# Two fp32 one-hots instead of one bf16 one-hot in the edge loop of the third graph layer

## The reference

```
z = h @ W_func.T
e = leaky_relu(concat(z[edge_src], z[edge_dst], w) @ W_att.T, 0.01)
m = segment_max(e, edge_dst)
alpha = exp(e - m[edge_dst]);  alpha /= segment_sum(alpha, edge_dst)
agg = segment_sum(alpha[:, None] * z[edge_src], edge_dst)
h_new = relu(h @ W_self.T + agg)          # h itself for nodes without an edge
x = x + h + h_new
```

## Time and profile before

| what | value |
|---|---|
| median of 3 runs | 8807.85 us (8803.87 to 8810.25) |
| profiled execution, its own time | 8805.21 us |
| its span | 8803.1 us |
| mean granted TensorE clock | 0.83 |
| DVE busy over the span | 5511.9 us (63%) |
| POOL busy over the span | 5197.2 us (59%) |
| PE busy over the span | 5993.1 us (68%) |
| ACT busy over the span | 3064.8 us (35%) |

### The profile page before, as it was taken

The page is one execution under the profiler, slowest core; times in us unless marked ns, Lnnn a source line. Parts: engine busy times, 40 slices in busy tenths (PEclk is TensorE's granted clock), DMA queues, the critical chain, the costliest instruction groups (busy, mean ns, idle before and its releaser), DMA issues. The chain is left out here.

```text
span 8803.1 us, 115446 instructions
## 1 busy us (share of the span) xinstructions
PE 5993.1 (68%) x29150; PEld 4494.9 (51%) x29150; DVE 5511.9 (63%) x14431; ACT 3064.8 (35%) x8921; POOL 5197.2 (59%) x5085
## 2 busy tenths in 40 slices
PE   0266787775259766656598999974477775574499
PEld 0133555553248534444477777763355553453487
DVE  8787888887656566665544434346577777435444
ACT  0111888886422210000233333321244444313322
POOL 0274666665567667777577777742677771433422
PEclk9687999998579987777699989877689886786699
DMA  9412655665147533333111111116433344463364
GB/s 303 152 52 80 172 172 170 175 174 150 37 152 213 163 99 101 101 102 102 35 28 30 26 29 31 26 27 200 115 103 104 104 102 116 155 214 91 115 199 163
DMA packets 655611, 1031.12 MB, mean 117 GB/s; under 512 B 134978, under 2 KB 462066, under 8 KB 654780
## 3 DMA queue, kind: packets, MB, share of 16 engines
q0 software_dynamic: 238656, 527.35, 22.3%
q1 hardware_dynamic: 390636, 444.00, 16.0%
q10 hardware_dynamic: 25744, 53.10, 2.0%
HBM read 806.11 MB, written 225.75 MB: 117 GB/s over the span
## 5 line engine op out<-in xcount | busy, mean ns | idle before, releaser
L4092 POOL DMA_INDIRECT gat_edges_rows<-gat_table,gat_room x1080 | 1171.4, 1085 | 366.4 <-issue 327.9
L2570 POOL DMA_INDIRECT l_edges_ring<-pairs,first_room x832 | 841.8, 1012 | 525.6 <-issue 243.1
L2132 POOL DMA_INDIRECT l_sum_rows<-l_feats,back_room x832 | 826.7, 994 | 279.8 <-issue 241.9
L2152 PE MATMUL l_sum_o<-l_sum_rows,l_sum_s 128*128 128x256 f32 x1664 | 616.2, 532 | 442.3 <-DVE l_sum_s L2163 206.2
L2621 ACT ACTIVATE l_edges_ring<-l_edges_ring,l_edges_weight 128x64 f32<-128x64 f32 x3328 | 816.5, 336 | 0.0
L2152 PEld LDWEIGHTS l_sum_o<-l_sum_rows,l_sum_s 128*128 128x128 f32 x1664 | 416.3, 264 | 635.8 <-DVE l_sum_s L2163 306.6
L2693 PE MATMUL l_edges_o<-l_edges_ring,l_edges_sf 128*128 128x260 f32 x1664 | 534.5, 427 | 148.8 <-DVE l_acc L2826 140.9
L3723 ACT ACTIVATE m_ffn_ht<-m_ffn_hp,m_ffn_b1t 128x256 f32<-128x256 f32 x592 | 280.7, 475 | 868.4 <-PE m_ffn_hp L3691 868.1
L2174 DVE TENSOR_TENSOR l_acc<-l_acc,l_sum_o 128x256 f32 x832 | 350.0, 421 | 346.6 <-PE l_sum_o L2152 256.6
L3701 PE MATMUL m_ffn_yp<-m_ffn_w2b,m_ffn_ht 128*128 128x256 f32 x2368 | 546.6, 384 | 29.2 <-ACT m_ffn_ht L3723 28.5
L3691 PE MATMUL m_ffn_hp<-m_ffn_xt,m_ffn_w1b 128*128 128x256 f32 x2368 | 548.7, 385 | 5.8 <-DVE m_ffn_xt L3738 3.0
(11 more groups left out here) (868 smaller groups left out, 14612.4 us busy)
## 6 DMA issues: line engine op xcount, KB each, us to landing
sorted_rows<-count_main_zero ACTq DMA_DIRECT2D x1, 51858.0 KB, 237.8
l_proj_taken<-m_by_node SPq DMA_DIRECT2D x56, 768.0 KB, 7.4
m_ffn_xs<-sorted_rows SPq DMA_DIRECT2D x144, 258.0 KB, 3.5
m_ffn_w1b<-in_L_ffn_w SPq DMA_DIRECT2D x32, 1024.0 KB, 6.2
m_ffn_w2b<-in_L_ffn_w SPq DMA_DIRECT2D x32, 1024.0 KB, 5.1
m_ffn_w1b<-in_L_ffn_W SPq DMA_DIRECT2D x56, 512.0 KB, 4.5
m_ffn_w2b<-in_L_ffn_W SPq DMA_DIRECT2D x56, 512.0 KB
m_by_node<-gat_edges_ys SPq DMA_DIRECT2D x96, 256.0 KB
```

Of the source, the lines that this page charges most:

```text
L2132: pool.indirect_dma_start(rows[:, slot, j, :], None, table, bass.IndirectOffsetOnAxis(ap=L.src[:, t:t + 1], axis=0)).then_inc(got[slot], 16)
L2152: pe.matmul(o[:, j, 0:D], s4[:, q % S4, j, :], rows[:, slot, j, :], start=True, stop=True).then_inc(out_done, 1)
L2570: pool.indirect_dma_start(rows(q, 0, 2 * D)[:, j, :], None, table, bass.IndirectOffsetOnAxis(ap=L.src[:, t:t + 1], axis=0)).then_inc(got[q ...
L4092: pool.indirect_dma_start(rows[:, slot, j, :], None, table, bass.IndirectOffsetOnAxis(ap=L.src[:, q * B + j:q * B + j + 1], axis=0)).then_ ...
```

## The change

The ring `s8` goes. In its place stand `early`, two slots in fp32, and `late`, four slots in fp32. Together they take as many bytes as `s8` did (12 slots of 2 bytes an element against 6 of 4 bytes). VectorE now makes each quad's one-hot twice: `first_onehot`, lag 2, into `early`, for `exclude`; and `second_onehot`, lag 7, into `late`, for `turn_s` and `weigh_s`. `turn_s` reads the upper halves of the fp32 words as bf16 (1.0 and 0.0 lie there whole), which is every other 2-byte element. `first_onehot` waits for the mask of two quads before, `second_onehot` for the weighing of four quads before. A semaphore `late_ready` is added.

In VectorE's step s the order of the plain functions is now: `second_onehot(s-7)`, `first_onehot(s-2)`, `score(s-2)`. Before it was: `score(s-2)`, `onehot(s)`. The generators follow in both.

```diff
-        s8 = ph.sb("s8", [P, U, B, P], BF16)
+        SA, SB = 2, 4
+        early = ph.sb("early", [P, SA, B, P])
+        late = ph.sb("late", [P, SB, B, P])
+        late_high = late[:].rearrange("p s b k -> p (s b k)").bitcast(BF16).rearrange(
+            "p (s b k half) -> p s b k half", s=SB, b=B, k=P, half=2)[:, :, :, :, 1]
...
+        late_ready = ph.sem("late_ready")
...
-                    act.activation(far[:, q % 2], s8[:, slot], ACT.Identity, bias=minus_far[:],
+                    act.activation(far[:, q % 2], early[:, q % SA], ACT.Identity, bias=minus_far[:],
                                    scale=FAR).then_inc(far_ready, 1)
...
                     act.wait_ge(ex_ready, q + 1)
+                    act.wait_ge(late_ready, q + 1)
...
-                        act.activation(ws[:, q % 2, j, :], s8[:, slot, j, :], ACT.Identity,
+                        act.activation(ws[:, q % 2, j, :], late[:, q % SB, j, :], ACT.Identity,
                                        scale=ex[:, q % 2, j, :]).then_inc(ws_ready, 1)
...
-                    pe.wait_ge(s_ready, q + 1)
+                    pe.wait_ge(late_ready, q + 1)
...
-                        ins = pe.transpose(stp[:, j, :], s8[:, slot, j, :], core.ident_b[:])
+                        ins = pe.transpose(stp[:, j, :], late_high[:, q % SB, j, :], core.ident_b[:])
...
-                def onehot(q, slot):
-                    if q >= U:
-                        dve.wait_ge(ws_ready, (q - U + 1) * B)
-                    dve.tensor_tensor(s8[:, slot], bc(core.row[:], 1, [P, B, P]),
-                                      bc(L.dst[:, q * B:(q + 1) * B], 2, [P, B, P]), ALU.is_equal).then_inc(s_ready, 1)
+                def onehot(out, q):
+                    return dve.tensor_tensor(out, bc(core.row[:], 1, [P, B, P]),
+                                             bc(L.dst[:, q * B:(q + 1) * B], 2, [P, B, P]), ALU.is_equal)
+
+                def first_onehot(q, slot):
+                    if q >= SA:
+                        dve.wait_ge(far_ready, q - SA + 1)
+                    onehot(early[:, q % SA], q).then_inc(s_ready, 1)
+
+                def second_onehot(q, slot):
+                    if q >= SB:
+                        dve.wait_ge(ws_ready, (q - SB + 1) * B)
+                    onehot(late[:, q % SB], q).then_inc(late_ready, 1)
...
-                steps(dve, n, [(0, onehot), (2, score), (2, split), (4, update), (5, refresh), (9, exponent),
+                steps(dve, n, [(2, first_onehot), (7, second_onehot), (2, score), (2, split), (4, update), (5, refresh), (9, exponent),
                                (10, add)], **whole)
```

## The result

The changed kernel takes 8821.08 us (median of 20 runs, 8805.09 to 8829.89), the kernel before 8803.28 us (20 runs, 8792.74 to 8814.38). The ratio is 1.0017, with a 95% interval of 1.001 to 1.0023: slower by 0.17%, or 17.8 us between the medians; the interval is 9 to 20 us. The forecast was 8831 us, +26 us, in a range of 8806 to 8872.

The account below looks back on a forecast made before the run. The prediction took POOL's back-to-back gathers as the bound. Gather delays of +23 us and a tail of +3 us, +26 us on the profiled execution's 8805.21 us, gave 8831 us, range 8806 to 8872 (own range 8818 to 8850).

Parts of the forecast that it names:

- The bound: In the loop, POOL issues gathers back to back, DVE follows the landed rows and the other engines follow DVE.
- A second comparison is free on DVE: The added one-hot's 1.13 us a step lies under DVE's 2.0 us wait for rows before `score`.
- The fp32 output, ScalarE's fp32 reads and the strided loads at nothing: fp32 one-hots on DVE, `exclude` and `weigh_s` on ACT, `turn_s` weight loads on PE: each taken as 0 us.
- One gather's wait per pair, to the end of the first one-hot: A gather starting inside the first one-hot ends 0.82 us behind that one-hot's end; one delay per pair.
- 0.55 us a step for even phases: Mean gather delay from a pair in the loop, against 0.31 before; over 97 steps +23 us.
- The part for gathers held through a pair: Within the delay per pair: 2 in 82 gathers held 1.3 us longer, adding 0.03 us.
- the second rival: Port held through the whole pair in one of four kinds of step: +46 us on top, 8877 us; chance 0.14.
- The tail: Behind the last gather, five more steps make a `second_onehot`: +3 us, between 0 and 5.7.
- DVE's wait for rows, 1.2 us a step: DVE's wait before `score` in the loop was to fall from 2.0 to about 1.2 us a step.
- without the one-hot inside (1.13): Removing the one-hot behind `score` shortens that part of DVE's step by 1.13 us; two in front add 2.26.
- The fourth rival: DVE becomes the bound if its steps grow by more than 1.3 us; 8900 us with 2 us more; chance 0.03.
- rival 1: Pairs meet gathers at kind phases, delay 0.25 to 0.45 us a step; 8802 to 8822 us, say 8812; chance 0.26.

Follow-up runs that it names:

- pair_behind: Changed kernel with both fp32 one-hots issued directly behind `score` instead of in front; 8822.92 against 8821.96 us for the kernel before, ratio 1.0003.
- one_ahead: Kernel before with its single bf16 one-hot moved to lag 2, in front of `score`; 8827.69 against 8821.96 us, ratio 1.0000.
- bf16_pair: Changed kernel with both one-hots in bf16, so `turn_s` loads contiguous weights; 8833.73 against 8821.96 us for the kernel before, ratio 1.0013.
- by_tile: Kernel before with its single 1024-element comparison made as eight short `tensor_scalar` comparisons of 128 elements; 8794.36 against 8821.96 us, ratio 0.9969.
- three_in_front_3: Changed kernel with `first_onehot` computed twice in a row, three comparisons in front of `score`; 8834.24 against 8807.41 us for the kernel before, ratio 1.0032.
- by_tile_three_2: Kernel before with comparisons made tile by tile in `edge_softmax`, `edge_sum` and `gat_edges`; 8775.89 against 8807.41 us, ratio 0.9964.

## Why the prediction came out right

Its mechanism is the one that the traces show. That the total came so near is in part luck: the terms that can be read from the trace add up to +13 us and not +26, and the timed runs say 17.8.

**The bound.** Right. GpSimd's gathers set the pace in both kernels, and no wait of POOL for `val_ready` appeared.

**A second comparison is free on DVE.** Right behind the score: `pair_behind` has it and takes before's time. In front of the score the trace says the same, for `one_ahead` has no second comparison and its gathers wait as long as the changed kernel's; the times leave some us open. The loss is of place, not of work. The fp32 output, ScalarE's fp32 reads and the strided loads at nothing: right (`bf16_pair`).

By the half of the Trainium skill's rule that I set aside (SBUF — State Buffer, "Who interferes with whom": descriptor writing isn't blocked by `tensor_tensor`), `by_tile` would have gained nothing; it gained 27.6 us.

**One gather's wait per pair, to the end of the first one-hot.** Right: 94 of 101 gathers show it, and a pair costs one wait. The term of the sum, 0.55 us a step for even phases, was too large: 46.6 us over 104 steps are 0.45. The phases weren't even; in two of the four kinds of step 18 of 48 pairs began 1.0 to 1.15 us ahead of a gather, where little or nothing is left to wait for. The term comes to +14 us, not +23. The part for gathers held through a pair (0.03 us, and the second rival) measured nothing.

**The tail.** Predicted +3 us, measured -0.5 in the profiled executions. DVE waits less there than before: 2.3 us for rows where it was 9.3, and 8.5 us for `collect` where it was 11.9. That covers the 5.7 us of one-hots.

**DVE's wait for rows, 1.2 us a step.** Wrong: 0.35. The step that failed is "without the one-hot inside (1.13)": taking the one-hot from behind the score didn't free 1.13 us, since 0.55 us a step of register loads had been hidden behind it. It cost no time only because DVE isn't the bound. DVE's own step was predicted nearly right, 9.29 us, where `three_in_front_3` gives 9.4: the loads hide again as soon as DVE is late. The fourth rival was about 1.0 us a step away, where I had counted 1.3.

**The rivals.** The kindly phase (rival 1) came in part: 0.45 us a step is the upper edge of its range. The result, 8821 us, lies both in the forecast's own range (8818 to 8850) and in rival 1's (8802 to 8822), just under the line of 0.2%. The number alone doesn't decide between them.

## What to carry to other kernels

Where GpSimd issues indirect DMAs back to back and sets the pace, look at when each of VectorE's long instructions starts against a gather's start; the price of a comparison here was what was left of it at that moment, less 0.13 us, and not its length. A second one directly behind the first cost the gathers nearly nothing, and making it in short pieces was even a gain, as long as the engine itself isn't at its limit. Before an instruction is moved from behind a wait to in front of it, ask what the engine's queue did beside it: the register loads that it covered came into the open here. All this was measured on chips on which the kernel takes 8800 to 8825 us.

## What the runs showed that I had not expected

- Register loads of 0.7 us behind a wait for rows, seen as "issue": 66 us in 960 in the changed kernel, 15 before, 71 with the single one-hot moved, 6 with the pair behind the score.
- Two ways in which a gather meets a row of VectorE instructions. If it starts inside one, it goes on at that one's end, even if the next has begun (94 of 101). If it starts 0.01 us ahead of the row, beside a small comparison that is still running, it can be held to the row's end: 3.92 us for sixteen instructions of 0.2 us. That moment alone doesn't decide: in `gat_edges` all 41 gathers of the kernel before that began 0.01 to 0.02 us ahead of the pair beside `gat_edges_first` were held, but in `edge_softmax` the 2 that began 0.01 us ahead of a one-hot beside `update`'s maximum (in `one_ahead` and `bf16_pair`) were free, like the 14 that began 0.02 to 0.03 us ahead. And in `by_tile_three_2` 13 of 15 gathers were held that began 0.57 to 0.58 us into the row, 0.01 us ahead of its fourth instruction. What makes the difference stays open; it wasn't tried by itself.
- The same programs on two other chips took 10600 to 10950 us, with gathers as short as here (940 to 950 ns in the median) but long waits for "issue" between them. Gains and losses of some tenths of a per cent didn't carry over to them.
